# A graph network's second spline convolution: the node pass reads two of the three table slots, and ScalarE copies the base rows

## The chip, the cores and the metric

The kernel runs on one core of a Trainium2 chip. The metric is the device time of one execution in microseconds. Before the change the median of three runs is 1833.41 us (1830.89 to 1840.7).

## What is computed

The input is a graph with N = 50000 nodes of 64 channels and E = 25000 edges, sorted by their target node. Three edge passes follow each other: two spline convolutions and one attention layer.

```
h = relu(layernorm(x))
conv(h): msg[e] = sum of 4 of 25 weight matrices applied to h[src[e]]
         agg[n] = max of msg over the edges that end in n, 0 where none ends
         return agg + h @ root + bias
h1 = relu(conv1(h));  x1 = x + conv2(h1)
out = x1 + attention(relu(layernorm(x1)))
```

For a node in which no edge ends, agg is zero, and its attention term is zero too. Such a node's output is x + h1 @ root2 + bias2.

## The kernel before

**The table.** A tensor T1 in device memory holds three slots of U = 68 floats (272 bytes) for every node, ROW = 3U = 204 floats (816 bytes) in all. Slot 0 holds conv 1's maximum, scattered there for the nodes in which an edge ends and zero for all others. Slot 1 holds conv 1's base row (h @ root1 + bias1) and slot 2 holds x. conv 1's hidden row of a node is relu(slot 0 + slot 1).

**Groups.** Conv 2 runs over G = 49 groups. A group is 512 edges in four tiles of 128, and at the same time 1024 nodes, 8 on each of 128 partitions. The last group has 848 nodes, on 106 partitions. Each engine has its own hand-written step(g); steps of neighbouring groups overlap, and the loop in the middle is unrolled four times.

**The edge pass.** GpSimd gathers the rows of both ends of the 512 edges, all three slots of each, in eight indirect DMAs a group (L581), into one of four buffers. VectorE adds slots 0 and 1 of the ends (sum_ends, L1309), spreads them over the spline knots (spread_z, L1328), and TensorE transposes that (turn_z, L973) and multiplies by the weights (product_pair, L980). ScalarE evacuates the transposes with a relu (evacuate, L762), VectorE weighs the products (weigh, L1348), adds them up and runs the segmented maximum (scan, L1340). TensorE turns messages and maxima (L1000, L1048). For the ends, TensorE transposes the rows (turn_ends, L1031), ScalarE applies the relu (L779), TensorE multiplies by root2 (end_roots, L1039) and VectorE finishes the base rows of the ends (base_out, L1404 and L1406). A node in which an edge ends gets its final output later, in the attention pass, which scatters whole rows over the output (L588).

**The node pass.** It writes x + h1 @ root2 + bias2 for all nodes of a group, and the attention pass overwrites the rows of the nodes in which an edge ends. SP loads the table rows of group g + 1 in step g into nt, two buffers by parity (L508). VectorE adds slots 0 and 1 into nh (node_in, L1382), TensorE transposes nh (turn_nodes, L1011), ScalarE applies the relu into nhT (L802), TensorE multiplies by root2 (node_roots, L1022), and VectorE adds slot 2 and the bias (node_out, L1391 and L1394). SP stores the result (L500).

**Order on the engines in a step of conv 2.** TensorE: product_pair(g, 0), turn_ends(g), turn_z(g, 2), turn_messages(g - 1), turn_z(g, 3), end_roots(g), turn_nodes(g), turn_z(g + 1, 0), product_pair(g, 1), turn_z(g + 1, 1), node_roots(g), turn_back(g - 1). VectorE: weigh 0, sum_ends(g + 1), spread_z 0 and 1, weigh 1, node_in, scan(g - 1), base_out, spread_z 2, weigh 2, spread_z 3, weigh 3, the sums, node_out. ScalarE: the gather indices for g + 3 (L684), the relu of the ends (L779), evacuate(g, 2), the copy of the ids (L784), evacuate(g, 3), the relu of the nodes (L802), evacuate(g + 1, 0) and (g + 1, 1), the copy of the maxima's rows (L814). SP: stores of group g - 2's maxima rows (L493) and of the output of g - 1 (L500), the load of g + 1 (L508), the transposed maxima of g - 1 (L513), the cut row of g + 1 (L449), the base rows of the ends of g (L519).

**The relations around the change.** Group g's nh may be written when turn_nodes(g - 1) has read it (npe, "nt"), and turn_nodes(g) waits for nh (xn) and for the relu of the ends, which reads the same PSUM bank. The load into nt waits until nh of two groups before was made (xn) and slot 2 was added (out, "acc").

Of the kernel before, what the change touches and what calls it, by code (L numbers as in the profile page):

```python
# [103 lines left out]
def wait(eng, steps, g, name=None):  # L104

    value = steps.at(g, name)
    if not isinstance(value, int) or value > 0:
        eng.wait_ge(steps.sem, value)

def wait_fill(eng, sems, g, per):

    value = g.uses(per, len(sems))
    if not isinstance(value, int) or value > 0:
        eng.wait_ge(sems[g.slot(len(sems))], value)

def build(nc, a, out):
# [17 lines left out]
    with ExitStack() as ctx:  # L136
# [113 lines left out]

        conv_mem = Arena()
        nx = [conv_mem.take([P, NPP, U]) for _ in (0, 1)]
        nt = [conv_mem.take([P, NPP, ROW]) for _ in (0, 1)]
        no = [conv_mem.take([P, NPP, U]) for _ in (0, 1)]
        nln, nq, nh = (conv_mem.take([P, NPP, C]) for _ in range(3))
        mlp_mem = Arena(conv_mem.at)
# [148 lines left out]
        def _(sp):  # L405
# [82 lines left out]
            def step2(g):  # L488
                if (g - 2).within(G):
                    n = g - 2  # L490
                    wait(sp, t["row"], n)
                    sp.sem_inc(sp_gate, 1)
                    sp.dma_start(M2[bass.ds(n.from_end(G, EG, 1), EG)].rearrange("(t p) c -> p t c", p=P),  # L493
                                 srow[n.slot(SLOTS)][:, :, 0:C]).then_inc(t["mstore"][n.parity], 16)
                if (g - 1).within(G):
                    n = g - 1
                    wait(sp, t["out"], n, "out")
                    sp.sem_inc(sp_gate, 1)
                    rows, p = node_rows(out, n)
                    sp.dma_start(rows, no[n.parity][0:p, :, 0:C]).then_inc(t["nstore"][n.parity], 16)  # L500
                if (g + 1).within(G):
                    n = g + 1
                    wait(sp, t["xn"], n - 2)
                    sp.sem_inc(sp_gate, 1)
                    wait(sp, t["out"], n - 2, "acc")
                    sp.sem_inc(sp_gate, 1)
                    rows, p = node_rows(T1n, n)
                    sp.dma_start(nt[n.parity][0:p], rows).then_inc(t["nload"][n.parity], 16)  # L508
                if (g - 1).within(G):
                    n = g - 1  # L510
                    wait(sp, t["agg"], n)
                    sp.sem_inc(sp_gate, 1)
                    sp.dma_start(MT2[:, bass.ds(n.from_end(G, EG), EG)], agg[n.parity]).then_inc(t["tstore"][n.parity], 16)  # L513
                if (g + 1).within(G):
                    load_ends(t, g + 1)
                if g.within(G):
                    wait(sp, t["base"], g, "out")
                    sp.sem_inc(sp_gate, 1)
                    sp.dma_start(B2[bass.ds(g.from_end(G, EG), EG)].rearrange("(t p) c -> p t c", p=P),  # L519
                                 be[g.parity]).then_inc(t["bstore"][g.parity], 16)  # L520
# [133 lines left out]
        def _(act):  # L654
# [98 lines left out]
            def conv(n):  # L753
                s = cs[n]

                def step(g):
                    def evacuate(g, j):

                        wait(act, s["turn"], g, f"t{j}")

                        first, chunks = (0, 2) if j % 2 == 0 else (2, 3)
                        act.activation(ZT[j // 2][:, first:first + chunks, :], bank[j % 2][:, 0:chunks * P], ACT.Relu)\  # L762
                            .then_inc(s["zt"].sem, 1)

                    if n == 1 and (g + 3).within(G, 2):
                        gidx1(g + 3)
                    if n == 2 and (g + 3).within(G, SLOTS):
                        gidx2(g + 3)
                    if n == 1 and (g - 1).within(G):
                        e = g - 1  # L770
                        wait_fill(act, s["scattered"], e - SLOTS, 16 * TPG)
                        act.activation(sidx[e.slot(SLOTS)][:, :], back_tiles_of(thirdI, e), ACT.Copy)\
                            .then_inc(s["sidx"].sem, 1)
                        act.activation(srow[e.slot(SLOTS)][:, :, C], back_tiles_of(rowI, e), ACT.Copy)\
                            .then_inc(s["rowid"].sem, 1)
                    if n == 2 and g.within(G):
                        wait(act, s["et"], g)
                        wait(act, s["er"], g - 1)
                        act.activation(ehT[:, :], bank[6][:, :], ACT.Relu).then_inc(s["ets"].sem, 1)  # L779
                    if g.within(G):  # L780
                        evacuate(g, 2)
                    if n == 2 and g.within(G):
                        wait_fill(act, s["gathered"], g, 32 * TPG)
                        act.activation(back_tiles_of(idxI, g), gath[g.slot(SLOTS)][:, :, 0, C], ACT.Copy)\  # L784
                            .then_inc(s["idx"].sem, 1)
                    if n == 1 and (g + 2).within(G):
                        wait(act, s["ecen"], g + 2)
                        wait(act, s["evar"], g + 1)
                        act.activation(lnq[:, 0:TPG, :], lnc[:, half_of(g), :], ACT.Square)\
                            .then_inc(s["esq"].sem, 1)  # L790
                    if n == 1 and (g + 1).within(G):
                        wait(act, s["ncen"], g + 1)
                        wait(act, s["nvar"], g)
                        act.activation(nq[:, :, :], nln[:, :, :], ACT.Square).then_inc(s["nsq"].sem, 1)
                    if n == 1 and g.within(G):
                        wait(act, s["npe"], g, "nt")
                        act.activation(nhT[:, :], bank[6][:, :], ACT.Relu).then_inc(s["nts"].sem, 1)
                    if g.within(G):
                        evacuate(g, 3)
                    if n == 2 and g.within(G):  # L800
                        wait(act, s["npe"], g, "nt")
                        act.activation(nhT[:, :], bank[6][:, :], ACT.Relu).then_inc(s["nts"].sem, 1)  # L802
                    if n == 1 and ((g + 1).within(G) or (g + 2).within(G)):
                        wait(act, s["norm"], g + 2, "eps")
                        act.activation(jst[:, 4, :], jst[:, 2, :], ACT.Sqrt).then_inc(s["root"].sem, 1)
                    if (g + 1).within(G):
                        evacuate(g + 1, 0)
                        evacuate(g + 1, 1)
                    if (g - 1).within(G):
                        e = g - 1  # L810
                        wait(act, s["at"], e)
                        if n == 2:
                            wait_fill(act, s["mstore"], e - 2, 16)
                        act.activation(srow[e.slot(SLOTS)][:, :, 0:C],  # L814
                                       bank[5][:, 0:TPG * C].rearrange("p (t c) -> p t c", c=C), ACT.Copy)\
                            .then_inc(s["row"].sem, 1)

                each(act, step, 3, 1, ahead=3)
# [324 lines left out]
        def _(dve):  # L1143
# [147 lines left out]
            def conv(n):  # L1291
# [78 lines left out]
                        .then_inc(s["comb"].sem, 1)  # L1370

                def node_in(g):
                    if n == 1:
                        wait(dve, s["norm"], g + 1, "rstd")
                        wait(dve, s["npe"], g - 1, "nt")
                        V_.tensor_tensor(nh[:, :, :], nln[:, :, :],
                                         jy[:, TPG:].unsqueeze(2).broadcast_to([P, NPP, C]), ALU.mult)\
                            .then_inc(s["xn"].sem, 1)
                    else:
                        wait_fill(dve, s["nload"], g, 16)  # L1380
                        wait(dve, s["npe"], g - 1, "nt")
                        V_.tensor_tensor(nh[:, :, :], nt[g.parity][:, :, 0:C], nt[g.parity][:, :, U:U + C], ALU.add)\  # L1382
                            .then_inc(s["xn"].sem, 1)

                def node_out(g):
                    wait(dve, s["npe"], g, "nr")
# [1 line left out]
                    r = bank[7][:, :].rearrange("p (t c) -> p t c", c=C)  # L1388
                    o = no[g.parity][:, :, 0:C]
                    if n == 2:  # L1390
                        V_.tensor_tensor(o, r, nt[g.parity][:, :, 2 * U:2 * U + C], ALU.add).then_inc(s["out"].sem, 1)  # L1391
                        wait(dve, s["out"], g, "acc")
                        r = o
                    V_.tensor_tensor(o, r, bias[n - 1][:, :].unsqueeze(1).broadcast_to([P, NPP, C]), ALU.add)\  # L1394
# [62 lines left out]
                def step(g):  # L1457
# [26 lines left out]
                        centre_rows(e)  # L1484
                    if now:
                        weigh(g, 1)
                        if n == 2:
                            node_in(g)
                    if (g - 1).within(G):
                        scan(g - 1)  # L1490
                    if now and n == 2:
# [156 lines left out]
```

## Time and profile before

| | before |
|---|---|
| median of three runs | 1833.41 us (1830.89 to 1840.7) |
| span of the profiled execution | 1831.4 us |
| TensorE busy (matmul) | 1524.8 us, 83% |
| VectorE busy | 1481.5 us, 81% |
| GpSimd busy | 1228.0 us, 67% |
| ScalarE busy | 732.2 us, 40% |
| DMA moved | 232.10 MB in 408085 packets |
| conv 2 | about 694 to 1268 us of the span |

The span runs from the first to the last instruction of one execution; it is one of the times that the median is made of, and lies close to it. PE is TensorE's matmuls, PEld its weight loads, which overlap them, DVE is VectorE, ACT is ScalarE, POOL is GpSimd, SP is the engine that issues plain DMAs; a q behind a name is the engine's sequencer. L12 is line 12 of the kernel.
### The profile page before, as it was taken

The numbers are of one execution on the slowest core, as the hardware profiler recorded it, in microseconds if no ns is written. First come the engines' busy times: TensorE is split into PE (matmuls) and PEld (weight loads), VectorE is DVE, ScalarE is ACT, GpSimd is POOL, SyncE is SP. The second block draws the span as 40 slices with busy tenths as digits, with TensorE's granted clock in tenths as the row PEclk, the third lists the DMA queues.
The fourth block names the chain that finished last, engine by engine and source line by source line (L and its number), as shares of the span: only waits on it lengthen the run. The fifth ranks groups of instructions, "written<-read, shape, count | busy, mean of one in ns | idle before, by whom it ended". The sixth has DMA issues, their size and how long they took to land.

```text
span 1831.4 us, 33936 instructions
## 1 busy us (share of the span) xinstructions
PE 1524.8 (83%) x7745; PEld 989.1 (54%) x7745; DVE 1481.5 (81%) x2831; ACT 732.2 (40%) x1841; POOL 1228.0 (67%) x1207
## 2 busy tenths in 40 slices
PE   2977888888888986999999999997777767667764
PEld 1264566566656665777777777775443334334432
DVE  3688999999999985999999999986777667666664
ACT  2463333333333323323322333223655545554553
POOL 4004777777777757777777777751577777777776
PEclk8588999999999997999999999998999999998998
DMA  5993444444444534887777777773233332333230
GB/s 99 164 110 65 101 104 107 100 106 101 106 105 101 106 73 124 242 233 231 228 225 221 227 227 226 233 221 88 60 80 67 80 67 68 69 77 69 67 73 19
DMA packets 408085, 232.10 MB, mean 127 GB/s; under 512 B 305989, under 2 KB 381958, under 8 KB 408046
## 3 DMA queue, kind: packets, MB, share of 16 engines
q1 hardware_dynamic: 311730, 151.97, 31.2%
q0 software_dynamic: 44864, 65.52, 16.4%
q10 hardware_dynamic: 51452, 14.18, 6.1%
q8 instruction: 14, 0.23, 0.1%
q14 instruction: 25, 0.20, 0.0%
HBM read 141.71 MB, written 92.64 MB: 128 GB/s over the span
## 4 chain that ended last, share of the span: by engine, by line
PE 34%; POOL 11%; issue 8%; DVE 3%; DMA 3%; ACT 3%; POOLq 0%; DVEq 0%; ACTq 0%; SPq 0%
PE bank L980 17%; POOL gath L581 6%; POOL out_dram L588 6%; PE bank L973 3%; PE bank L1039 2%; PE bank L1022 2%; DMA gath<-M,gidx 2%; PE bank L1101 2%; PE bank L1011 2%; PE bank L1031 1%; PE bank L1000 1%; PE bank L1048 1%; DMA arena<-T 1%; PE bank L1120 1%; DVE arena L1570 1%
## 5 line engine op out<-in xcount | busy, mean ns | idle before, releaser
L980 PE MATMUL bank<-Wk,arena 128*128 128x320 f32 (+1 forms) x2352 | 657.6, 465 | 56.9 <-ACT arena L762 56.9
L980 PEld LDWEIGHTS bank<-Wk,arena 128*128 128x128 f32 (+1 forms) x2352 | 328.0, 189 | 304.6 <-issue 223.3
L581 POOL DMA_INDIRECT gath<-T,gidx x392 | 387.1, 988 | 146.9 <-issue 111.1
L581 POOL DMA_INDIRECT gath<-in_x_dram,gidx x196 | 197.3, 1007 | 161.1 <-ACT gidx L679 102.3
L581 POOL DMA_INDIRECT gath<-M,gidx x196 | 213.5, 1089 | 124.9 <-issue 55.8
L762 ACT ACTIVATE arena<-bank 128x256 f32<-128x256 f32 (+1 forms) x392 | 169.6, 433 | 308.3 <-PE bank L973 307.8
L588 POOL DMA_INDIRECT T<-srow,sidx x196 | 214.6, 1095 | 79.4 <-issue 66.8
L1348 DVE TENSOR_TENSOR arena<-bank,A 128x320 f32<-128x320 f32 x392 | 191.6, 489 | 66.4 <-PE bank L980 59.2
L588 POOL DMA_INDIRECT out_dram<-srow,sidx x196 | 199.8, 1019 | 61.3 <-issue 60.7
L973 PE MATMUL bank<-ident,arena 128*128 128x128 f32 x980 | 171.7, 274 | 10.6 <-DVE arena L1328 10.5
L973 PEld LDWEIGHTS bank<-ident,arena 128*128 128x128 f32 x980 | 124.6, 142 | 41.5 <-issue 7.3
L1340 DVE TENSOR_TENSOR_SCAN arena<-ends_cut,arena,bank 64x512 f32<-64x512 bf16 x98 | 123.8, 1263 | 0.3 <-PE bank L1000 0.3
L1120 PE MATMUL bank<-lnq,means 128*128 128x512 f32 x98 | 54.6, 639 | 75.5 <-ACT lnq L892 75.5
L1101 PE MATMUL bank<-arena,Wqk 128*128 128x512 f32 x98 | 60.8, 705 | 57.5 <-DVE arena L1558 57.5
L1022 PE MATMUL bank<-rootpair,nhT 128*128 128x128 f32 x784 | 103.5, 275 | 0.0
L1094 PE MATMUL bank<-DT,spread 128*128 (+1 forms) x392 | 101.9, 383 | 0.0
L1558 DVE SCALAR_TENSOR_TENSOR arena<-bank,arena 128x512 f32<-128x512 f32 x49 | 33.9, 692 | 82.2 <-ACT arena L899 82.2
L1022 PEld LDWEIGHTS bank<-rootpair,nhT 128*128 128x128 f32 x784 | 95.4, 192 | 0.3
L1328 DVE TENSOR_TENSOR arena<-lnc,a0r 128x320 f32<-128x320 f32 x196 | 93.6, 479 | 0.0
L779 ACT ACTIVATE arena<-bank 128x512 f32<-128x512 f32 x49 | 29.3, 598 | 155.7 <-PE bank L1031 155.7
L1094 PEld LDWEIGHTS bank<-DT,spread 128*128 128x128 f32 x392 | 71.8, 194 | 28.8 <-issue 23.4
L875 ACT ACTIVATE arena<-bank 128x512 f32<-128x512 f32 x49 | 29.3, 597 | 145.0 <-PE bank L1111 145.0
(185 smaller groups left out, 2738.8 us busy)
## 6 DMA issues: line engine op xcount, KB each, us to landing
arena<-T SPq DMA_DIRECT2D x48, 816.0 KB
T<-arena SPq DMA_DIRECT2D x96, 272.0 KB
T<-zero ACTq DMA_DIRECT2D x1, 13281.2 KB, 103.9
B<-arena SPq DMA_DIRECT2D x49, 256.0 KB
arena<-B SPq DMA_DIRECT2D x49, 256.0 KB, 3.8
arena<-in_x_dram SPq DMA_DIRECT2D x48, 256.0 KB, 4.1
out_dram<-arena SPq DMA_DIRECT2D x48, 256.0 KB, 3.5
begins_cut<-begins_d SPq DMA_DIRECT2D x49, 128.5 KB, 3.5
```

The costliest lines, as they stand in the source:

```text
L581: pool.indirect_dma_start(out=gath[slot][:, j, k, 0:width], out_offset=None, in_=table, in_offset=bass.IndirectOffsetOnAxis(gidx[slot][:, ...
L588: pool.indirect_dma_start(out=table, out_offset=bass.IndirectOffsetOnAxis(sidx[g.slot(SLOTS)][:, j:j + 1], 0), in_=srow[g.slot(SLOTS)][:, ...
L762: act.activation(ZT[j // 2][:, first:first + chunks, :], bank[j % 2][:, 0:chunks * P], ACT.Relu)\
L973: tr = pe.transpose(bank[j % 2][:, c * P:c * P + P], Z[g.parity][:, j // 2, (first + c) * P:(first + c + 1) * P], ident[:, :])
L980: return pe.matmul(bank[2 + r][:, 0:KO], ZT[q][rows, chunk, :], Wk[n - 1][rows, weights].rearrange("p k o -> p (k o)"), start=start, stop= ...
L1022: mm = pe.matmul(bank[7][:, q * P:q * P + P], nhT[:, q * P:q * P + P], root[n - 1][:, :], start=True, stop=True)
L1094: pe.matmul(bank[b + e.parity].rearrange("p (t h e) -> p h t e", h=2, e=P)[:, j], spread[:, j, :], pairs, start=(j == 0), stop=False, skip ...
L1101: pe.matmul(bank[b + g.parity][:, :], W[:, :, :].rearrange("p t c -> p (t c)"), XT[g.parity][:, :], start=False, stop=True, skip_group_che ...
L1120: pe.matmul(bank[7][:, :], means[:, :], squares, start=True, stop=True).then_inc(at["var"].sem, 1)
L1328: V_.tensor_tensor(Z[g.parity][:, j // 2, at_:at_ + KO].rearrange("p (k c) -> p k c", c=C), row.broadcast_to([P, K, C]), w.unsqueeze(2).br ...
L1340: V_.tensor_tensor_scan(agg[g.parity][:, ::-1], ends_cut[g.parity][:, ::-1], bank[4][0:C, ::-1], agg[1 - g.parity][:, 0:1], ALU.add, ALU.max)\
L1348: V_.tensor_tensor(V[:, j].rearrange("p (k o) -> p k o", o=C), bank[2 + j % 2][:, 0:KO].rearrange("p (k o) -> p k o", o=C), A1[:, bass.ds( ...
```

## The change

Conv 2's node pass leaves out slot 0. The load takes slots 1 and 2 of each node, 2U = 136 floats (544 bytes) of the 816, so its source is a run of 544 bytes for each node instead of one run of 6528 bytes for each partition. The buffer nt keeps its place and size, and is viewed as 8 rows of 2U floats. node_in on VectorE is left to conv 1 alone. In conv 2, ScalarE copies slot 1 from nt to nh, behind the relu of the ends and ahead of evacuate(g, 2), and carries the two waits that node_in had. node_out takes x from its new place. The nodes in which an edge ends get a different base row in the output at this point (without their maximum); the attention pass overwrites exactly these rows.

```diff
--- before.py
+++ after.py
@@ -250,7 +250,7 @@
 
         conv_mem = Arena()
         nx = [conv_mem.take([P, NPP, U]) for _ in (0, 1)]
-        nt = [conv_mem.take([P, NPP, ROW]) for _ in (0, 1)]
+        nt = [conv_mem.take([P, NPP * ROW])[:, 0:NPP * 2 * U].rearrange("p (t u) -> p t u", u=2 * U) for _ in (0, 1)]
         no = [conv_mem.take([P, NPP, U]) for _ in (0, 1)]
         nln, nq, nh = (conv_mem.take([P, NPP, C]) for _ in range(3))
         mlp_mem = Arena(conv_mem.at)
@@ -505,7 +505,7 @@
                     wait(sp, t["out"], n - 2, "acc")
                     sp.sem_inc(sp_gate, 1)
                     rows, p = node_rows(T1n, n)
-                    sp.dma_start(nt[n.parity][0:p], rows).then_inc(t["nload"][n.parity], 16)
+                    sp.dma_start(nt[n.parity][0:p], rows[:, :, U:ROW]).then_inc(t["nload"][n.parity], 16)
                 if (g - 1).within(G):
                     n = g - 1
                     wait(sp, t["agg"], n)
@@ -777,6 +777,9 @@
                         wait(act, s["et"], g)
                         wait(act, s["er"], g - 1)
                         act.activation(ehT[:, :], bank[6][:, :], ACT.Relu).then_inc(s["ets"].sem, 1)
+                        wait_fill(act, s["nload"], g, 16)
+                        wait(act, s["npe"], g - 1, "nt")
+                        act.activation(nh[:, :, :], nt[g.parity][:, :, 0:C], ACT.Copy).then_inc(s["xn"].sem, 1)
                     if g.within(G):
                         evacuate(g, 2)
                     if n == 2 and g.within(G):
@@ -1370,17 +1373,11 @@
                         .then_inc(s["comb"].sem, 1)
 
                 def node_in(g):
-                    if n == 1:
-                        wait(dve, s["norm"], g + 1, "rstd")
-                        wait(dve, s["npe"], g - 1, "nt")
-                        V_.tensor_tensor(nh[:, :, :], nln[:, :, :],
-                                         jy[:, TPG:].unsqueeze(2).broadcast_to([P, NPP, C]), ALU.mult)\
-                            .then_inc(s["xn"].sem, 1)
-                    else:
-                        wait_fill(dve, s["nload"], g, 16)
-                        wait(dve, s["npe"], g - 1, "nt")
-                        V_.tensor_tensor(nh[:, :, :], nt[g.parity][:, :, 0:C], nt[g.parity][:, :, U:U + C], ALU.add)\
-                            .then_inc(s["xn"].sem, 1)
+                    wait(dve, s["norm"], g + 1, "rstd")
+                    wait(dve, s["npe"], g - 1, "nt")
+                    V_.tensor_tensor(nh[:, :, :], nln[:, :, :],
+                                     jy[:, TPG:].unsqueeze(2).broadcast_to([P, NPP, C]), ALU.mult)\
+                        .then_inc(s["xn"].sem, 1)
 
                 def node_out(g):
                     wait(dve, s["npe"], g, "nr")
@@ -1388,7 +1385,7 @@
                     r = bank[7][:, :].rearrange("p (t c) -> p t c", c=C)
                     o = no[g.parity][:, :, 0:C]
                     if n == 2:
-                        V_.tensor_tensor(o, r, nt[g.parity][:, :, 2 * U:2 * U + C], ALU.add).then_inc(s["out"].sem, 1)
+                        V_.tensor_tensor(o, r, nt[g.parity][:, :, U:U + C], ALU.add).then_inc(s["out"].sem, 1)
                         wait(dve, s["out"], g, "acc")
                         r = o
                     V_.tensor_tensor(o, r, bias[n - 1][:, :].unsqueeze(1).broadcast_to([P, NPP, C]), ALU.add)\
@@ -1484,8 +1481,6 @@
                         centre_rows(e)
                     if now:
                         weigh(g, 1)
-                        if n == 2:
-                            node_in(g)
                     if (g - 1).within(G):
                         scan(g - 1)
                     if now and n == 2:
```

## Rows read from the trace of the kernel before

**Rows 1.** Windows: length, busy PE, PEld, DVE, ACT, POOL (x), PEclk, DMA share, GB/s.

```profile
752.00:1232.00 480.00, 479.94 (x2855) 345.95 (x2854) 434.84 (x779) 147.37 (x432) 343.73 (x350) 1.00 0.79 229
1232.00:1276.00 44.00, 33.40 (x183) 23.33 (x181) 30.70 (x51) 13.42 (x29) 0.45 (x1) 0.87 0.32 90
```

**Rows 2.** Chain of waits, one steady group (start us, us, engine, tile, line).

```profile
996.03 0.44 PE bank L1031 x4
...
998.34 0.57 PE bank L1011 x4
...
1007.12 0.44 PE bank L1031 x4
```

**Rows 3.** Chain of waits, a group in which turn_nodes waits for nothing.

```profile
740.25 0.44 PE bank L1031 x4
...
742.56 0.44 PE bank L1011 x4
...
751.20 0.44 PE bank L1031 x4
```

**Rows 4.** Timeline of a steady group (start us, us, engine, line, operation; idle before).

```profile
1006.06 0.61 SPq L500 DMA_DIRECT2D out_dram<-arena  x1
...
1007.17 0.37 SPq L508 DMA_DIRECT2D arena<-T  x1
...
1007.59 0.60 ACT L779 ACTIVATE arena<-bank 128x512 f32<-128x512 f32 x1 [3.08 <-PE bank L1031]
...
1008.08 0.38 ACT L762 ACTIVATE arena<-bank 128x256 f32<-128x256 f32 x1
...
1008.54 0.68 DVE L1382 TENSOR_TENSOR arena<-arena 128x512 f32<-128x512 f32 x1
...
1009.33 0.42 PEld L1011 LDWEIGHTS bank<-ident,arena 128*128 128x128 f32 x4
...
1009.83 0.38 PE L973 MATMUL bank<-ident,arena 128*128 128x128 f32 x2
...
1010.03 0.60 ACT L802 ACTIVATE nhT<-bank 128x512 f32<-128x512 f32 x1 [0.97 <-PE bank L1011]
1010.05 3.25 PE L980 MATMUL bank<-Wk,arena 128*128 128x320 f32 x12
```

**Rows 5.** Waits in the steady stretch, 752 to 1232 us (us, times, longest).

```profile
POOL gath L581 <- ACT gidx L684: 32.0, 37, 1.2
DVE arena L1348 <- PE bank L980: 27.1, 86, 0.4
```

**Rows 6.** Timeline of the last group.

```profile
1240.15 0.37 SPq L508 DMA_DIRECT2D arena<-T  x1
...
1250.19 2.94 SPq L500 DMA_DIRECT2D out_dram<-arena  x1
...
1252.95 0.49 ACT L762 ACTIVATE arena<-bank 128x384 f32<-128x384 f32 x1
1255.82 0.69 DVE L1382 TENSOR_TENSOR arena<-arena 128x512 f32<-128x512 f32 x1 [3.80 <-DMA arena<-T]
...
1256.66 0.63 PE L1011 MATMUL bank<-ident,arena 128*128 128x128 f32 x4 [2.85 <-DVE arena L1382]
...
1257.12 4.86 PE L980 MATMUL bank<-Wk,arena 128*128 128x320 f32 x12
```

**Rows 7.** ScalarE in conv 1, by form: busy us, mean ns, idle.

```profile
L794 ACT ACTIVATE arena<-arena 128x512 f32<-128x512 f32 x44 | 27.7, 629 | 8.7 <-DVE arena L1438 8.7
```

**Rows 8.** The gathers of conv 2, by form.

```profile
L581 POOL DMA_INDIRECT gath<-T,gidx x338 | 333.1, 986 | 127.7 <-issue 95.6 <-ACT gidx L684 32.0
```

**Rows 9.** DMA packets while the last load runs alone, 1247.8 to 1248.8 us.

```profile
q1 hardware_dynamic: 8, 0.05, 12.4%
```

**Rows 10.** DMA packets of the last store of the output, 1267.2 to 1271.8 us.

```profile
q1 hardware_dynamic: 566, 0.14, 14.7%
```

**Rows 11.** DMA packets of conv 1's last stores to the table, 683 to 692 us.

```profile
q1 hardware_dynamic: 782, 0.21, 14.5%
```

## Prediction

> **What bounds the kernel now.** The change touches conv 2 alone, so I read that stage first. The windows by stage show it as 480 us of steady loop (752 to 1232 us of the span) in which TensorE is busy 479.94 us at a granted clock of 1.00, VectorE 434.84 us, ScalarE only 147.37 us, and the DMA engines 79% [rows 1]. VectorE is loaded at 91%, but a busy share alone doesn't say who waits. The chain of waits does: through a steady group it runs from TensorE to TensorE without leaving it. One group takes 1007.12 - 996.03 = 11.09 us [rows 2]. The reader should look for the one piece that is longer than its work. Four transposes back to back take 0.44 us (L1031); turn_nodes (L1011) is the same four transposes and takes 0.57 us [rows 2]. In a group where nothing makes it wait it is 0.44 us too, and that group takes 751.20 - 740.25 = 10.95 us [rows 3]. So 0.13 us of each steady group is a wait, and it is the only one on TensorE that I find.
>
> The timeline says for what. node_in on VectorE (L1382) starts at 1008.54 and ends 0.68 us later, at 1009.22; the weight load of turn_nodes starts at 1009.33 [rows 4]. I followed the pair through all 49 groups: from group 3 to group 46, and in group 1, the weight load comes 0.10 to 0.11 us after node_in's end. In groups 0, 2 and 47 node_in is early and the gap ahead of turn_nodes is the ordinary 0.11 us. That makes 45 groups with this wait. The view of waits doesn't list it, as it is put down to "issue"; it does show VectorE waiting for TensorE's products instead, 86 times and 27.1 us in all, two times a group [rows 5]. VectorE is therefore not the bound: its share is high because it follows TensorE closely.
>
> The last group is different. node_in waits 3.80 us for the table rows, which were asked for at 1240.15 and let it start at 1255.82; turn_nodes waits 2.85 us behind it, and the twelve product instructions after that take 4.86 us, against 3.25 us for twelve in a steady group [rows 4, 6]. The granted clock over 1232 to 1276 is 0.87 on average [rows 1].
>
> **Removed from VectorE: node_in, 49 x 0.68 us = 33 us of busy time** [rows 4]. This is the large number, and nearly all of it is off the path. What lies on the path is TensorE's wait for it: 45 x 0.13 us = 5.9 us. What is late next: TensorE's own queue. With no wait a group takes 10.95 us [rows 3], all of it back-to-back issue, so the gain can't exceed 0.14 us in a steady group. That the rest of VectorE's time is freed only lengthens its waits for L980.
>
> **Added to ScalarE: a copy of 128x512 from SBUF to SBUF, 49 x 0.63 us = 31 us.** The price is that of the nearest row, conv 1's square of the same shape and memory, 629 ns [rows 7]; the other end is the 0.60 us of the same size out of PSUM [rows 4]. Where it stands matters more. It goes behind the relu of the edge ends (L779, start 1007.59) and ahead of evacuate(g, 2). The next ScalarE instruction started 0.49 us after that relu began [rows 4], so the copy runs from about 1008.08 to 1008.71, and turn_nodes, which can start at 1009.26 at the earliest, finds its rows ready with 0.45 us to spare after the 0.10 us of signalling. Queued behind the copy are evacuate(g, 2), the copy of the ids, evacuate(g, 3) and the relu of the nodes. Each slips by about 0.5 us, or 0.65 us if the two new waits cost something. evacuate(g, 2) would end at 1009.0 to 1009.1 instead of 1008.46; its reader, turn_z(g+1, 0), starts at 1009.83 now and at 1009.70 then [rows 4]. evacuate(g, 3) ends near 1009.6 and is read by the third product of product_pair(g, 1), over a microsecond later. The node relu starts at 1010.03 now and its reader is node_roots, 3 us on. So the copy costs nothing as long as it stays under about 1.1 us; above that TensorE would wait for bank 0 at turn_z. The ids for the gathers come at the start of the step, well before. GpSimd waits for them, 32.0 us in 37 waits [rows 5], but it catches up (eight gathers at 0.99 us and some 0.3 us of issue between them are 10.3 us [rows 8]), so a group of 10.95 us is within its reach.
>
> **The new wait on ScalarE is for the load of the table rows.** The load of group g+1 is issued at 1007.17 [rows 4], and the copy would want it at about 1019.2, 12 us later. By the signals of the trace the 48 full loads land 4.3 to 7.7 us after issue, the median 6.1, and VectorE's node_in is not among those that wait in the steady stretch [rows 5]. Spare: over 4 us.
>
> **The load changes shape: 1024 pieces of 544 bytes with gaps instead of 128 runs of 6528 bytes.** Two thirds of the bytes, eight times the pieces. No row shows a piece of 544 bytes, so I bound it. A 6528-byte packet takes 0.124 x 16 x 1.0 us / 8 = 248 ns [rows 9]; a 256-byte one 0.147 x 16 x 4.6 us / 566 = 19.1 ns [rows 10]; a 272-byte one beside scatters 0.145 x 16 x 9.0 us / 782 = 26.7 ns [rows 11]. A straight line through the first two gives 29.6 ns for 544 bytes, one through the first and third 36.3 ns; by bytes alone it would be 20.7 ns. I take 29.6 ns, since its short packets belong to the same stage and the same kind of moment. Steady state: 1024 x 29.6 = 30 us of engine time a group, against 128 x 248 = 32 us. The DMA share stays at or just under 0.79, and nothing moves. SP would issue for 0.61 us instead of 0.37 us per load, the price of L500 with its 1024 pieces [rows 4], and SP has time.
>
> The Trainium skill speaks against this edit: Perfetto Trace Analysis, DMA Optimizations, holds that transfers under 2 KB carry a significant overhead each and that batching them up is the first thing to do. The rows agree that small packets are dearer per byte (19.1 ns for 256 bytes, 248 ns for 6528, which is about twice per byte), and here a third fewer bytes pay for that.
>
> **The last group's load goes over two engines.** 106 partitions are left, and during that load the 16 engines together are busy 12.4%, which is two of sixteen [rows 9]. Each of the two moves 53 packets: 53 x 248 ns = 13.1 us of the 15.65 us. New: 424 x 29.6 ns = 12.6 us, so it lands 0.6 us sooner. Bounds: by bytes alone 8.8 us (4.3 us sooner), by the dearer line 15.4 us (2.3 us later). The copy is 0.05 us shorter than node_in. Here the order on ScalarE matters, since evacuate(48, 2) and (48, 3) now stand behind a copy that waits for the load; before, both were long done, at 1252.95 + 0.49 [rows 6]. After landing L: copy to L + 0.65, evacuate 2 to about L + 0.9, evacuate 3 to L + 1.5; the products start at L + 1.3 and want the third chunk after L + 2.2. Covered. SP may be held too: with hundreds of pieces outstanding on two engines, the next transfers' issues stretch, as L500's does to 2.94 us [rows 6]. Behind it stand the maxima, the cut row and the base rows of groups 47 and 48; the first reader, the scan of group 48, comes about 10 us after the landing. Hidden. I count the last group at -0.6 us. The slow clock that follows the stall stays, as the stall stays.
>
> **Sum.** -5.9 - 0.6 = -6.5 us. The profiled execution spans 1831.4 us, 2.0 us under the median of the runs (1833.41), so I subtract from the median: 1826.9 us, 0.35% less.
>
> **Rivals.**
> *Another wait takes its place* (gain 0 to 2 us, 1832 us). For it: end_roots starts directly as the relu of the ends is done (1007.59 + 0.60 = 1008.19), with hardly any slack, and ScalarE's queue gets longer. Against: that relu stands ahead of the copy, and turn_z has half a microsecond of cover. 12%.
> *The last load no longer holds anything up* (1823.0 us). 848 pieces divide by sixteen; if they went over sixteen engines, the load would land in some 5 us, the 2.85 us wait would vanish, and perhaps the 1.6 us of slow clock behind it: -5.9 - 2.85 - 1.6 = -10.4 us. Against: conv 1's last stores have the same shape on both sides and also run at the share of two engines, 14.5% [rows 11]. 10%. The Trainium skill, DMA: Bandwidth & Descriptors (Why a DMA increments its semaphore by 16 and not by 1), says that the count of engines is the largest number up to 16 that divides the outermost size of both sides. With 106 partitions on the SBUF side that is two in both kernels, and the rows of two-engine shares agree with it.
> *The pieces bind the DMA engines* (slower). The group's engine time is 0.79 x 16 x 11.09 = 140 us [rows 1], of which the load is 32 us; room at 10.95 us a group is 175 us, so the 1024 pieces may cost up to (175 - 108) / 1024 = 65 ns each. Beyond that it decides. At 80 ns a group takes (108 + 82) / 16 = 11.9 us, 0.8 us more in 49 groups, and the last load takes 34 us instead of 13: 1833 + 40 + 21 = 1894 us. For it: these are reads at a pitch of 816 bytes among gathers of the same table. Against: the dearest short packet of the trace is 26.7 ns, and twice that is still under the limit. 7%. A milder form, the last load alone 3 us later, lies inside the range of the forecast.
>
> **How the numbers follow.** The forecast has 71%: 1826.9 us, by itself from 1822.5 to 1832 us (4.3 us sooner or 2.3 us later in the last load, half of the steady gain lost). With the first two rivals, and the runs' own spread (1830.89 to 1840.7 before), the range is 1820 to 1836 us; it leaves out the DMA bound. A measurement of this kernel can tell about 0.5% (9.2 us) from no change. Over 0.5% faster needs the second rival, or the good ends of both terms: 13%. Over 0.5% slower: 8%. Within: 79%.
>
> **What would show it.** Right: turn_nodes' four transposes take 0.44 us in a steady group of about 10.95 us; VectorE's waits for L980 grow by about 0.6 us a group; the copy takes 0.6 us and starts 0.5 us after the relu of the ends; the last group's wait of TensorE is still 2 to 3 us. Wrong: any wait of L973 for ScalarE; the copy waiting for the load in a steady group; a DMA share over 0.9 in the loop; a last wait under 1 us or over 5 us.

## The result and the profile after

| | before | after |
|---|---|---|
| median of five runs | 1833.41 us | 1821.99 us |
| runs | 1830.89 to 1840.7 | 1821.01 to 1826.17 |
| span of the profiled execution | 1831.4 us | 1820.2 us |
| mean steady group of conv 2 (40 groups) | 11.118 us | 10.988 us |
| TensorE's wait in the last group | 2.85 us | 1.17 us |

The ratio is 0.9941, with a 95% interval from 0.9922 to 0.9959: 10.8 us faster (7.5 to 14.3), where 6.5 us were forecast. (Five runs were timed on each side, not three.) The busy times at the head of the page after:

```profile
PE 1524.3 (84%) x7745; PEld 992.4 (55%) x7745; DVE 1452.5 (80%) x2782; ACT 752.1 (41%) x1890; POOL 1235.5 (68%) x1207
```

VectorE is 29 us less busy and ScalarE 20 us more. Neither number is what the time did. The chain of waits through one steady group is (start us, us, engine, tile, line; L1014 after is L1011 before, L1034 is L1031, L1042 is L1039):

```profile
992.98 0.44 PE bank L1034 x4
...
994.40 0.89 PE bank L1042 x8
995.29 0.44 PE bank L1014 x4
995.73 0.22 PE bank L976 x2
```

turn_nodes takes 0.44 us, as in the group that waited for nothing [rows 3] and not 0.57 us as in a steady one [rows 2]. The timeline of another group shows why (start us, us, idle before in brackets):

```profile
1004.03 0.61 SPq L508 DMA_DIRECT2D arena<-T  x1
...
1004.41 0.60 ACT L779 ACTIVATE arena<-bank 128x512 f32<-128x512 f32 x1 [3.15 <-PE bank L1034]
...
1004.91 0.62 ACT L782 ACTIVATE arena<-arena 128x512 f32<-128x512 f32 x1
...
1005.43 0.38 ACT L762 ACTIVATE arena<-bank 128x256 f32<-128x256 f32 x1
...
1005.98 0.47 PEld L1014 LDWEIGHTS bank<-ident,arena 128*128 128x128 f32 x4
...
1006.53 0.38 PE L976 MATMUL bank<-ident,arena 128*128 128x128 f32 x2
```

The copy (L782) ends at 1005.53, 0.45 us ahead of the weight load of turn_nodes, and evacuate(g, 2) (the first L762) ends at 1005.81, 0.72 us ahead of its reader (L976). Neither reader waits. Three groups in four take 10.96 us, and the fourth 11.08 us, which gives the mean of 10.988 us. The waits of the steady stretch name what VectorE does with its freed time:

```profile
DVE arena L1351 <- PE bank L983: 49.1, 129, 0.5
```

It waits 49.1 us for TensorE's products in 476 us, where it waited 27.1 us in 480 us [rows 5]. In the windows the loop's clock and DMA share are as before [rows 1]: 1.00 and 0.79, at 206 GB/s instead of 229.

```profile
752.00:1228.00 476.00, 476.00 (x2864) 346.19 (x2863) 411.46 (x737) 166.61 (x478) 354.10 (x350) 1.00 0.79 206
```

These rows of the last group stand beside [rows 6]:

```profile
1234.26 0.78 SPq L508 DMA_DIRECT2D arena<-T  x1
...
1237.11 7.61 SPq L513 DMA_DIRECT2D MT<-arena  x1
...
1248.29 0.63 ACT L782 ACTIVATE arena<-arena 128x512 f32<-128x512 f32 x1 [1.64 <-DMA arena<-T]
...
1249.07 0.63 PE L1014 MATMUL bank<-ident,arena 128*128 128x128 f32 x4 [1.17 <-ACT arena L782]
...
1249.53 3.26 PE L983 MATMUL bank<-Wk,arena 128*128 128x320 f32 x12
```

The row of L513 before was

```profile
1243.58 0.50 SPq L513 DMA_DIRECT2D MT<-arena  x1
```

Counted to the instruction that waits for it, the load lands 14.0 us after its issue instead of 15.65 us, and the twelve product instructions behind the wait take 3.26 us instead of 4.86 us. The windows around those products, the first of the kernel before and the second of the one after (columns as in rows 1), show the clock:

```profile
1256.70:1261.80 5.10, 5.10 (x16) 2.76 (x17) 2.76 (x4) 0.60 (x1) 0.00 (x0) 0.67 0.32 87
```

```profile
1249.10:1253.30 4.20, 4.20 (x23) 2.85 (x24) 1.21 (x3) 1.16 (x4) 0.00 (x0) 1.00 0.41 111
```

Before, TensorE ran at a mean granted clock of 0.67 there (part of it at 1.2 GHz); after, at 1.00 (2.4 GHz throughout).

### The profile page after: what moved, and what is told of

Read it like the earlier page. It is cut to its first block, busy times and chain, and to the rows that moved or that the text cites. A ratio compares the mean times of both kernels' runs of the same rounds, so it can differ in the third digit from the quotient of the medians.

```text
span 1820.2 us, 33944 instructions
## 1 busy us (share of the span) xinstructions
PE 1524.3 (84%) x7745; PEld 992.4 (55%) x7745; DVE 1452.5 (80%) x2782; ACT 752.1 (41%) x1890; POOL 1235.5 (68%) x1207
## 4 chain that ended last, share of the span: by engine, by line
PE 35%; POOL 9%; issue 8%; DVE 4%; ACT 4%; DMA 3%; DVEq 0%; POOLq 0%; ACTq 0%; SPq 0%
PE bank L983 17%; POOL gath L581 5%; POOL out_dram L588 4%; PE bank L976 3%; PE bank L1042 2%; PE bank L1025 2%; PE bank L1104 2%; DMA gath<-M,gidx 2%; PE bank L1123 1%; PE bank L1014 1%; PE bank L1034 1%; PE bank L1003 1%; PE bank L1051 1%; DVE arena L1565 1%; DMA arena<-T 1%
## 5 line engine op out<-in xcount | busy, mean ns | idle before, releaser
L581 POOL DMA_INDIRECT gath<-T,gidx x392 | 396.6, 1012 | 130.9 <-issue 124.4
L762 ACT ACTIVATE arena<-bank 128x256 f32<-128x256 f32 (+1 forms) x392 | 168.5, 432 | 308.5 <-PE bank L976 308.5
L976 PE MATMUL bank<-ident,arena 128*128 128x128 f32 x980 | 171.7, 274 | 10.6 <-DVE arena L1331 10.5
L976 PEld LDWEIGHTS bank<-ident,arena 128*128 128x128 f32 x980 | 124.2, 142 | 41.7 <-issue 7.8
```

The lines of the kernel that those rows point to most:

```text
L581: pool.indirect_dma_start(out=gath[slot][:, j, k, 0:width], out_offset=None, in_=table, in_offset=bass.IndirectOffsetOnAxis(gidx[slot][:, ...
L976: tr = pe.transpose(bank[j % 2][:, c * P:c * P + P], Z[g.parity][:, j // 2, (first + c) * P:(first + c + 1) * P], ident[:, :])
```

## Experiments

**How they are read.** The ratios of whole runs have an interval of 0.1 to 0.2% to either side, 2 to 4 us, and most of the terms are of that size. Each trace also gives two sharper measures: the mean steady group, and the stretch from the first gather of conv 2 to the first gather of the attention pass, which holds all of conv 2 and its two ends. What follows is GpSimd's queue of gathers and scatters, which took 545.4 to 550.0 us from its first gather to its last scatter in the thirteen traces, without a clear order by kernel.

| kernel | steady group, us | first gather to first gather, us | ratio to before (95%) |
|---|---|---|---|
| before, two profiles | 11.118, 11.120 | 579.8, 580.4 | |
| the change, two profiles | 10.988, 10.988 | 569.7, 570.2 | 0.9941 (0.9922 to 0.9959), 0.9946 (0.9926 to 0.9966) |
| copy on ScalarE, three slots | 10.988 | 573.6 | 0.9969 (0.9954 to 0.9983) |
| addition on VectorE, two slots, two profiles | 11.122, 11.121 | 576.6, 576.7 | 0.9969 (0.9957 to 0.9981), 0.9966 (0.9952 to 0.9979) |
| copy on VectorE, two slots | 10.988 | 570.2 | 0.9951 (0.9935 to 0.9968) |
| before, last load cut | 11.119 | 575.2 | 0.9979 (0.9964 to 0.9994) |
| the change, last load cut | 10.988 | 568.4 | 0.9937 (0.9917 to 0.9958) |
| the change, all last transfers cut | 10.988 | 564.2 | 0.9919 (0.9900 to 0.9937) |
| the change, one copy more | 11.108 | 576.1 | one execution, no interval |
| the change, two copies more | 11.630 | 601.3 | one execution, no interval |

The diffs below are cut to the lines that matter, and what is left out is named beside each.

**Theory W** was formed on the traces of before and after: 45 waits of 0.13 us gone, and the last load sooner with the slow clock behind it gone. **Rival V**: VectorE's freed time counts. **Rival L**: the smaller load did it. **Rival J**: the rest of the kernel gained as well.

### The change again

No edit.

> The changed kernel once more, beside the others of this chip. Theory W (what the two traces show): 45 waits of TensorE for node_in gone, 0.127 us each, -5.8 us; last load lands 1.65 us sooner and the products behind it run at 3.26 us instead of 4.86 us for twelve, -3.3 us; together -9.1 us, ratio 0.9950. Rival J: another 2 us lie in the start of conv 2 and in the attention stage and belong to the change, ratio 0.9941 or less. If they are chance, turn_nodes to turn_nodes still is 10.96 us and the time lies 8 to 12 us under the kernel before.

Measured: 10.988 us a group, 0.9946, a time of 1822.42 us. From gather to gather it is 9.9 us shorter than the mean of the two profiles of before. The ratio lies between W's 0.9950 and J's 0.9941, and its interval holds both. J is taken up below and stays open.

### Each half alone

The copy moved, the load as it was (against the changed kernel; the view of nt and the place from which node_out takes x also go back to three slots):

```diff
-                    sp.dma_start(nt[n.parity][0:p], rows[:, :, U:ROW])
+                    sp.dma_start(nt[n.parity][0:p], rows)
-                        act.activation(nh[:, :, :], nt[g.parity][:, :, 0:C], ACT.Copy)
+                        act.activation(nh[:, :, :], nt[g.parity][:, :, U:U + C], ACT.Copy)
```

> The copy on ScalarE alone: the load still brings all three slots in 6528-byte runs. The maxima are left out of nh as in the changed kernel. Theory W: the steady part stays (a group takes 10.96 us, -5.8 us), the last load lands 15.6 us after its issue again, TensorE waits 2.8 us for it and the slow clock follows; -5.8 us in all, ratio 0.9968. Rival L (the smaller load did it, steady part too): a group takes 11.09 us, time as before. Rival V (VectorE's 33 us of freed time are worth more than the one wait): nothing changes against the changed kernel, ratio 0.994.

The steady part is all there, 10.988 us a group, with 6528-byte runs: rival L falls for it. The last group is that of before (timeline):

```profile
1250.68 0.63 ACT L782 ACTIVATE arena<-arena 128x512 f32<-128x512 f32 x1 [3.44 <-DMA arena<-T]
...
1251.45 0.63 PE L1014 MATMUL bank<-ident,arena 128*128 128x128 f32 x4 [2.98 <-ACT arena L782]
...
1251.92 4.85 PE L983 MATMUL bank<-Wk,arena 128*128 128x320 f32 x12
```

So the two terms are separate: a wait of 2.98 us, and 4.85 us for the products after it. Rival V, which wanted the changed kernel's full gain here, falls too: 573.6 us against 570.0. The ratio, 0.9969, is the 0.9968 expected.

The load alone, with an addition of the same size left on VectorE (it adds zeros, the maxima left out; against the kernel before; the view of nt, the load of slots 1 and 2 and the place of x are those of the change):

```diff
-                        V_.tensor_tensor(nh[:, :, :], nt[g.parity][:, :, 0:C], nt[g.parity][:, :, U:U + C], ALU.add)
+                        V_.tensor_tensor(nh[:, :, :], nt[g.parity][:, :, 0:C], zero[:, 0:C].unsqueeze(1).broadcast_to([P, NPP, C]), ALU.add)
```

> The load of two slots alone: VectorE keeps an addition of the same size at the old place (slot 1 plus a row of zeros, the maxima left out). Theory W: TensorE waits 0.13 us for it in each steady group as before (11.09 us a group), the last load lands 14.0 us after issue, the last wait is about 1.2 us and no slow clock follows it; -3.3 us, ratio 0.9982. Rival L: a group takes 10.96 us and the time is that of the changed kernel. Rival V: a group takes 11.09 us and the end of conv 2 is as before, ratio 1.000.

The chain shows the wait in its old place:

```profile
999.00 0.89 PE bank L1039 x8
999.89 0.57 PE bank L1011 x4
```

11.122 us a group, so rival L falls here too. The stretch is 3.5 us shorter: the end of conv 2 and nothing else, so rival V falls as well. TensorE's last wait is 1.10 us, and the products behind it take 3.25 us. The ratio, 0.9969, was better than the 0.9982 worked out, so the kernel was timed again:

> The load of two slots alone once more. Its first rounds gave 0.9969 where the working from the trace gives 0.9982, just outside the interval. Theory W: nearer 0.998 this time, and the two together hold 0.998. Rival: the smaller load brings another 2 us outside the steady part, then 0.997 again.

0.9966: the rival's number, 0.997, came again, and W's 0.998 did not. The traces agree with each other to 0.2 us and show no such gain in conv 2. The two halves' stretches add up, 6.5 + 3.5 = 10.0 us against 10.1 us for the whole change. That the whole runs of this half come out 2 to 3 us lower than its trace accounts for stays open: 0.9982 lies just outside both intervals. Its two profiles took 547.1 and 550.0 us for the attention pass, so no gain of that size shows there either.

### Is it ScalarE, or only the end of the row

Against the kernel before; the view of nt, the load and the place of x are those of the change:

```diff
-                        V_.tensor_tensor(nh[:, :, :], nt[g.parity][:, :, 0:C], nt[g.parity][:, :, U:U + C], ALU.add)
+                        V_.tensor_copy(nh[:, :, :], nt[g.parity][:, :, 0:C])
```

> Two slots loaded, and the copy done by VectorE at the old place of node_in (the maxima left out as in the changed kernel). Theory W (one wait of 0.13 us, not VectorE's load): a plain copy out of SBUF into SBUF needs 0.1 us less than the addition if it is to end in time; at 0.55 us or less TensorE does not wait and the time is that of the changed kernel; at the addition's 0.68 us nothing changes in the steady part, 11.09 us a group. Rival V (freeing VectorE is what counts): 11.0 us or more a group whatever the copy takes, as VectorE keeps most of the work.

The copy on VectorE takes 0.42 us where the addition took 0.68 us (by form):

```profile
L1382 DVE COPY arena<-arena 128x512 f32<-128x512 f32 x42 | 17.6, 418 | 0.0
```

It ends in time, turn_nodes takes 0.44 us, and a group takes 10.988 us, as with ScalarE. VectorE keeps 18 of the 29 us that node_in cost it in this stretch, and the gain from gather to gather is the same, 570.2 us. The ratio of 0.9951 can't be told from the change's. Rival V has nothing left. The Trainium skill says (Perfetto Trace Analysis, Optimizing Scalar/DVE Operations) that work which both engines can do is faster on VectorE where one of its performance modes applies, and that some of it may go to ScalarE where VectorE is saturated. For the copy the rows agree that VectorE is the faster, 0.42 us against ScalarE's 0.62 us, but none of them tells its mode. As VectorE wasn't the bound, the second part didn't arise.

One thing off the path moved: GpSimd's gathers of conv 2 take 986 ns each where VectorE adds [rows 8], with either load, about 1015 ns where ScalarE copies, and 1067 ns here. It cost the steady group nothing, 10.988 us in both kernels; why the gathers grow, no run was made to show.

### How much cover the copy has

One copy more, ahead of the one that matters, into a buffer that conv 2 doesn't use:

```diff
+                        act.activation(nq[:, :, :], nt[g.parity][:, :, 0:C], ACT.Copy)
                         act.activation(nh[:, :, :], nt[g.parity][:, :, 0:C], ACT.Copy).then_inc(s["xn"].sem, 1)
```

> The changed kernel with a second copy of the same size ahead of the one that TensorE waits for, on ScalarE. The prediction gave the place a cover of about 1.1 us. Copies start 0.49 us apart, so the rows are ready 1.1 us after the first began, and evacuate(g, 2) ends 1.0 us later than before the change. Expected: TensorE waits 0 to 0.1 us in turn_nodes again, a group takes 10.96 to 11.06 us. If the cover was misjudged, a group takes 11.3 us or more.

```profile
1007.46 0.89 PE bank L1043 x8
1008.35 0.57 PE bank L1015 x4
```

11.108 us a group, a little over the 11.06 us expected at most: the wait is back, 0.13 us as VectorE's was. The rows are ready 0.49 + 0.62 = 1.11 us after the first copy began, so the cover is 1.11 - 0.13 = 0.98 us, a little under the prediction's 1.1 us. It also runs out elsewhere: the prediction named turn_z and its bank as the first to wait, and it is turn_nodes that waits. turn_z still takes its plain 0.22 us behind it. With two copies more than the change:

> Two copies more than the changed kernel, ahead of the one that TensorE waits for. One copy more brought the wait of 0.10 us in turn_nodes back (11.108 us a group). Each further copy starts 0.49 us behind the one before, and nothing covers it now: turn_nodes waits 0.6 us, a group takes 11.6 us, some 25 us more in 49 groups than with two copies. If the chain through turn_z(g+1, 0) is added on top, up to 12.0 us a group.

```profile
986.53 0.62 ACT arena L783
987.15 0.53 ACT arena L784
987.67 0.14 issue
987.81 0.63 PE bank L1016 x4
```

11.630 us, as expected. The chain now runs through ScalarE's copies, and each microsecond of them is one of the kernel. The kernel as a whole took 1853.53 us.

### The last load, cut

106 partitions can be loaded as 96 and 10. On the changed kernel (the last copy also waits for the second part):

```diff
-                    sp.dma_start(nt[n.parity][0:p], rows[:, :, U:ROW]).then_inc(t["nload"][n.parity], 16)
+                    q = p if p == P else 96
+                    sp.dma_start(nt[n.parity][0:q], rows[0:q, :, U:ROW]).then_inc(t["nload"][n.parity], 16)
+                    if q < p:
+                        sp.dma_start(nt[n.parity][q:p], rows[q:p, :, U:ROW]).then_inc(s_rest, 16)
```

> The changed kernel with the last group's load cut in two DMAs, 96 and 10 partitions, so that it can go over more than two engines. Theory W: it lands within 6 us of its issue, TensorE's last wait (1.17 us) vanishes, SP is no longer held for 7.6 us at the transposed maxima of group 47; 1.2 to 1.7 us under the changed kernel. Rival: something else of group 48 is as late (the copy of the ids, the relu), or SP's hold was shielding the load from other transfers, and nothing moves.

The larger part lands 4.5 us after its issue, and the Trainium skill's rule (DMA: Bandwidth & Descriptors, Why a DMA increments its semaphore by 16 and not by 1) gives 96 partitions sixteen engines and 10 partitions ten. The landing, 4.5 us against 14.0 us over two, agrees that there are many more than two; no row counts them. SP isn't held any more:

```profile
1235.99 0.55 SPq L517 DMA_DIRECT2D MT<-arena  x1
```

TensorE waits for nothing in the last group, and the stretch is 1.6 us shorter than the changed kernel's, the size expected. In the whole runs it can't be told from it (0.9937 against 0.9941 and 0.9946).

The same cut on the kernel before, with its three slots and its addition:

> The kernel before with the last load alone cut into 96 and 10 partitions, all three slots, nothing else changed. Theory W: the last load lands in 6 us, TensorE's wait of 2.85 us and the slow products behind it (1.6 us) vanish; -4.4 us, ratio 0.9976, with 11.09 us a group as before. Rival: the slow clock at the end of conv 2 comes from the end of the stage and not from the wait, then -2.9 us.

The stretch falls by 4.9 us, where 4.4 us were expected, and the ratio is 0.9979, with 11.119 us a group. The products of the last group take 3.25 us:

```profile
1252.57 0.68 DVE L1388 TENSOR_TENSOR arena<-arena 128x512 f32<-128x512 f32 x1
...
1254.71 3.25 PE L984 MATMUL bank<-Wk,arena 128*128 128x320 f32 x12
```

So all that the smaller load brought at the end of conv 2 is to be had without touching the slots, and the slow clock on these products belongs to the wait, not to the end of the stage.

### All last transfers, cut

On the changed kernel, the same for conv 1's last two stores to the table, the last load and the last store of the output; whoever waited for these transfers also waits for their second parts.

> All transfers of 106 partitions that follow the last group of a convolution are cut into 96 and 10: conv 1's last two stores to the table, the last load, the last store of the output. Theory W carried on: at the end of conv 2 SP is held for 5.2 us at the transposed maxima behind the 106-partition store, and with it the store of the last maxima rows for which the gathers of the attention pass wait; they start some 4 us sooner, and if GpSimd's queue bounds that pass, the whole time falls by 3 to 5 us against the kernel with only the load cut, to 1817 to 1819 us. At the end of conv 1 the scatters end as late as the stores, so 0 to 1 us there. Rival: the first groups of the attention pass wait for the dense layer's last chunks anyway, and nothing is gained.

SP isn't held any more, and the gathers of the attention pass begin 4.5 us sooner than with the load alone cut (1259.36 against 1263.85). Conv 2 itself began 0.3 us sooner, within the 0 to 1 us expected of conv 1's stores, so 4.2 us lie behind it. In the timeline:

```profile
1254.86 0.52 SPq L527 DMA_DIRECT2D MT<-arena  x1
1255.57 1.42 SPq L501 DMA_DIRECT2D M<-srow  x1
...
1259.36 1.15 POOL L595 DMA_INDIRECT gath<-M,gidx  x1 [39.80 <-DMA M<-srow]
```

The issue of the maxima (MT) takes 0.52 us, where it took over 5 us behind the store of 106 partitions. Ratio 0.9919 (0.9900 to 0.9937), some 1818.8 us by the ratio against the 1817 to 1819 us expected; its six runs lie between 1815.72 and 1823.71 us with a median of 1820.9 us. Of the kernels tried it has the shortest conv 2 and the lowest ratio, though its interval meets that of the change.

### Before, once more

> The kernel before once more, for its profile: is the 549.7 us from the first gather of the attention pass to its last scatter (545.4 to 549.9 us in the nine others) its own, or chance? Theory W: chance; 545 to 550 us again, the steady group of conv 2 at 11.12 us, and the first gather at 1275 to 1277 us. Rival J (the change shortens the attention pass too): 549.5 us or more.

11.120 us a group, the first gather at 1276.67 us, 550.0 us from there to the last scatter. That is over the 549.5 us which I had set for rival J, so by the line drawn the attention pass may belong to it. But the changed kernel with its load cut gave 549.9 us and the second profile of the addition 550.0 us. The changed kernel's two profiles gave 547.7 and 548.3 us. A share of the attention pass of up to 2 us in the gain is neither shown nor excluded.

## Why the prediction was right, and what was mis-sized

**The bound and the wait: right.** The chain of waits named TensorE, one piece of it was 0.13 us too long, and that is what went: 11.118 - 10.988 = 0.130 us a group, 45 times that is 5.9 us, the forecast term. The reading that VectorE's 91% follows TensorE rather than bounds it holds in both directions: the freed time turned into waiting (about 0.5 us a group more for L980's products, where 0.6 us were forecast), and a copy on VectorE itself does the same.

**The price and place of the copy: right.** 0.62 us measured, 0.63 us taken; it starts 0.50 us after the relu's start, 0.49 us taken; it ends 0.45 us ahead of the weight load, 0.35 us after the signalling, where 0.45 us were worked out. The point from which it would cost was put at about 1.1 us and lies at 0.98 us. The wait that comes first there was named wrongly: it is turn_nodes waiting for its rows and not turn_z waiting for its bank. At one copy neither waits, so this didn't touch the forecast.

**The steady load: right.** No wait for it, DMA share 0.79 in both. Other work's packets took longer by about what the load saved.

**The last group: the term that was mis-sized.** Forecast 0.6 us, measured 3.3 us between the two traces of the result (on TensorE, from turn_nodes of group 46 to the last product). The last group of the second profile of before took 0.45 us longer than that of the first, so the mean over two profiles of each kernel is 3.6 us, and the same with the load alone. The term has two parts. The load: a 544-byte piece was priced at 29.6 ns from 256 and 6528 bytes. The DMA view of five microseconds in which it runs alone shows

```profile
q1 hardware_dynamic: 402, 0.22, 14.3%
```

402 pieces in 5.0 us on two engines, 24.9 ns each, and 27.8 ns over the whole load (11.8 us for 424). So it landed 1.65 us sooner, not 0.6 us, well inside the bounds given. The rate is what to take for a price: the share of 14.3% for two engines (12.5%) shows that packets overlap, and durations from shares count them twice. The 19.1 ns for 256 bytes came from a share of 14.7%; by the rate of the same row [rows 10] they are 2 x 4.6 / 566 = 16.3 ns, and the line through 248 ns then gives 26.9 ns for 544 bytes, which would have forecast 1.7 us.

The other part is the sentence "The slow clock that follows the stall stays, as the stall stays." That step failed. The stall shrank from 2.85 to 1.17 us, and the granted clock behind it was 1.00 instead of 0.67 on average: 1.6 us. The forecast had this amount in its numbers, but only in the rival in which the wait disappears. The kernels line up: with waits of 2.85 and 2.98 us the products took 4.86 and 4.85 us, with 1.10 and 1.17 us or none 3.25 to 3.26 us.

**The rivals.** Another wait in its place: none came. Sixteen engines: no, the load stayed on two, and most of that rival's gain came without it. Pieces that bind the DMA engines: 25 to 31 ns measured against a limit of 65 ns.

**The range and the chances.** The measured 1821.99 us is nearer to the second rival's 1823.0 us than to the forecast's 1826.9 us, and lies 0.5 us outside the forecast's own 1822.5 to 1832 us; only the range widened for the rivals holds it. The case over 0.5% faster had 13% and came (0.59%, and 0.54% the second time), not the one within 0.5% with its 79%. Of the signs, the last wait of 2 to 3 us was missed (1.17 us). So the loop was understood, and that the time lies in the range owes something to its width.

**The sum.** 5.9 + 3.6 = 9.5 us, where the traces have 10.1 us from gather to gather. The rest lies ahead of the first turn_nodes of conv 2, which comes 0.2 to 1.1 us sooner behind the first gather in the traces of the change, of the copy with three slots and of the copy on VectorE, and on average 0.5 us sooner in the two of the change. It varies from trace to trace, and no run was made for it. The ratio's 10.8 us fits with 9.5 as with 10.1 us.

## What to carry to other kernels

Take an edit's price from the one wait that it ends, not from the work that it moves: 33 us of VectorE's work were worth 5.9 us, and the same 5.9 us was to be had with an instruction 0.26 us shorter where it stood. Where a stall only shrinks, price what follows it at both levels of the clock, since the slow stretch can go before the stall does. And look at the last, odd-sized group by itself: cutting its transfers so that they spread was worth about as much as the loop's gain, in the kernel before as in the changed one.

## What was not expected of the hardware

A transfer of 106 partitions in these kernels doesn't only run on two engines, it can hold the queue that issues it: the next issue took 7.61 us in the changed kernel, when it came 2.9 us after the load, and 5.24 us behind the last store of the output:

```profile
1257.56 5.24 SPq L513 DMA_DIRECT2D MT<-arena  x1
```

Many small pieces made it worse: with 6528-byte runs the next issue took 0.50 us, and only the fifth was long, 2.94 us [rows 6]. With load and store cut into 96 and 10 partitions, the next issues took 0.55 and 0.52 us. Behind the load it cost nothing that a wait of the last group shows; behind the output's store it cost the attention pass 4.2 to 4.5 us of its start.
